# One program per engine across four phases, with the norm's scaling moved to ScalarE

## What is computed

```python
x = x + _L0_xattn_ref(_layernorm(x, axis=-1), ctx_4096, mask_BxSxS2_bk0, ...)   # 32 heads of 128
x = x + _L0_ffn_ref(_layernorm(x, axis=-1), ...)                                # 512 -> 1376 -> 512
x = x + _L1_xattn_ref(_layernorm(x, axis=-1), ctx_4096, ctx_4096, ...)          # 32 query, 8 key heads
x = x + _L1_ffn_ref(_layernorm(x, axis=-1), ...)                                # 512 -> 512, low-rank part
```

```python
def _layernorm(x, axis=-1, eps=1e-05):
    m = jnp.mean(x, axis=axis, keepdims=True)
    v = jnp.var(x, axis=axis, keepdims=True)
    return (x - m) / jnp.sqrt(v + eps)
```

## Time and profile before

| what | us |
| --- | --- |
| three runs | 1722.76, 1722.99, 1725.99 |
| median | 1722.99 |
| the profiled execution | 1721.07 |
| its span, first to last instruction | 1719.3 |
| TensorE busy | 1674.7 |
| VectorE busy | 875.0 |
| ScalarE busy | 647.2 |
| GpSimd busy | 683.0 |

### The profile page before, as it was taken

How to read it: one execution, slowest core, us unless ns; L and a number is a source line. 1 busy time by engine, 2 the same in 40 slices (tenths; PEclk the granted TensorE clock), 3 DMA queues, 4 the chain that set the end, 5 groups by cost and what they waited for, 6 DMA issues and landing times. The chain is left out here.

```text
span 1719.3 us, 26202 instructions
## 1 busy us (share of the span) xinstructions
PE 1674.7 (97%) x9420; PEld 1448.9 (84%) x9420; DVE 875.0 (51%) x1454; ACT 647.2 (38%) x1765; POOL 683.0 (40%) x481
## 2 busy tenths in 40 slices
PE   8999999999999999999989999799999999999997
PEld 7888888888888888888868886688898788888875
DVE  5543444434444344443454345656657556675674
ACT  6432223322233222332322222456556455664550
POOL 4622244322443324433253433445445444443524
PEclk9999999999999999999989999899999999999998
DMA  5110110101101011010011110101011110010011
GB/s 204 53 52 27 52 52 24 52 27 52 52 25 51 30 49 52 29 47 34 1 56 49 43 38 25 65 32 37 32 38 43 45 37 31 25 44 25 27 36 49
DMA packets 30899, 75.00 MB, mean 44 GB/s; under 512 B 5776, under 2 KB 10256, under 8 KB 30832
## 3 DMA queue, kind: packets, MB, share of 16 engines
q1 hardware_dynamic: 30832, 74.10, 12.5%
HBM read 71.99 MB, written 2.10 MB: 43 GB/s over the span
## 5 line engine op out<-in xcount | busy, mean ns | idle before, releaser
L934 POOL TENSOR_TENSOR x_probs<-x_probs,x_inv 128x512 f32<-128x512 f32 x64 | 66.6, 1041 | 461.9 <-DVE x_inv L781 461.9
L1763 POOL TENSOR_TENSOR g_swapped<-g_swapped,rawB 128x512 f32<-128x512 f32 x80 | 103.4, 1294 | 196.9 <-ACT g_swapped L1550 196.9
L637 ACT COPY x_pT<-banks 128x512 f32<-128x512 f32 x64 | 37.4, 586 | 335.6 <-PE banks L486 335.6
L55 PE MATMUL banks<-wtV_hi,cT_lo 128*128 128x256 f32 x512 | 145.3, 284 | 0.0
L57 PE MATMUL banks<-wtV_hi,cT_hi 128*128 128x256 f32 x512 | 144.9, 283 | 0.0
L56 PE MATMUL banks<-wtV_lo,cT_hi 128*128 128x256 f32 x512 | 144.8, 283 | 0.0
L789 DVE COPY x_k<-banks 128x512 f32<-128x512 f32 x60 | 41.5, 692 | 135.6 <-PE banks L57 135.6
L789 DVE COPY x_v<-banks 128x512 f32<-128x512 f32 x60 | 41.5, 692 | 127.7 <-PE banks L57 127.7
L55 PE MATMUL banks<-wtV_hi,g_att_lo 128*128 128x512 f32 x256 | 104.9, 410 | 0.0
L813 DVE TENSOR_TENSOR resid<-banks,resid 128x512 f32<-128x512 f32 x128 | 84.1, 686 | 40.0 <-PE banks L57 40.0
L629 ACT ACTIVATE x_probs<-x_probs,x_top 128x128 f32<-128x128 f32 x256 | 99.2, 390 | 13.1 <-DVE x_top L772 13.1
(11 more groups left out here) (229 smaller groups left out, 4911.7 us busy)
## 6 DMA issues: line engine op xcount, KB each, us to landing
rawV<-in_x_wV SPq DMA_DIRECT2D x16, 512.0 KB, 3.2
rawO<-in_x_wO SPq DMA_DIRECT2D x16, 512.0 KB, 4.0
rawO<-in_g_wQ SPq DMA_DIRECT2D x16, 512.0 KB, 3.2
rawV<-in_g_wO SPq DMA_DIRECT2D x16, 512.0 KB, 3.2
rawA<-in_x_wA SPq DMA_DIRECT2D x15, 512.0 KB, 4.6
rawB<-in_x_wB SPq DMA_DIRECT2D x15, 512.0 KB, 3.2
rawA<-in_f_gu SPq DMA_DIRECT2D x5, 512.0 KB, 3.5
rawB<-in_f_gu SPq DMA_DIRECT2D x5, 512.0 KB, 3.3
```

Of the source, the lines that this page charges most:

```text
L55: pe.matmul(out, w[1], x[0], start=start, stop=False)
L637: nc.scalar.copy(pT[:, j, :], banks[:, TURN_BANK + j, :]).then_inc(pT_ready, 1)
L934: pool.tensor_tensor(probs[:, part, :], probs[:, part, :], rows, ALU.mult).then_inc(probs_ready, 1)
L1763: pool.tensor_tensor(part, part, sin[:, :].unsqueeze(1).to_broadcast([P, HB, P]), ALU.mult)\
```

## The change

The four blocks become one. Each phase is now an object with one function per engine (`Phase`), and each engine runs the four functions in a row; there is no barrier between them. Waits across a border go by semaphores that one phase hands to the next as hooks. The norm's scaling is done by ScalarE (`normalise`, activation Identity with scale `rstd` and bias `shift`), and GpSimd computes `shift` = -mean * rstd in a third one-column instruction. The orders at the borders are written anew. The diff, leaving out changes of indentation and what only renames:

```diff
-    def reciprocal_std(self, pool, b):
+    def factors(self, pool, b):
...
+        pool.wait_ge(self.rstd_ready, b + 1)
+        pool.tensor_scalar(core.shift[:, one], core.moments[:, b, 0:1], core.rstd[:, one], -1.0, ALU.mult, ALU.mult)\
+            .then_inc(self.shift_ready, 1)
-    def add_rows(self, pool):
+    def add_row(self, pool, b):
...
+        pool.wait_ge(self.normed_ready, b + 1)
...
-    def scale(self, dve, b):
+    def normalise(self, act, b):
...
-        dve.tensor_scalar(core.normed[:, b % 2, :], core.resid[:, b, :], core.moments[:, b, 0:1],
-                          core.rstd[:, b:b + 1], ALU.subtract, ALU.mult).then_inc(self.normed_ready, 1)
+        core.nc.scalar.activation(core.normed[:, b % 2, :], core.resid[:, b, :], ACT.Identity,
+                                  bias=core.shift[:, b:b + 1], scale=core.rstd[:, b:b + 1]).then_inc(self.normed_ready, 1)
```

Border 1, from phase 1 to 2 (TensorE, ScalarE, VectorE, GpSimd), and the first chunk of phase 2 on TensorE:

```diff
-                pv(tail, 0, 1, PAIRS - 1)
-                pv(tail, 1, 1, PAIRS - 1)
...
-                norm.weave_tensor(pe, lambda b: output_batch(PAIRS, b))
+            first_head(0)
+            first_head(1)
+            pv(tail, 0, 1, PAIRS - 1)
+            first_head(2)
+            pv(tail, 1, 1, PAIRS - 1)
+            first_head(3)
+            pe.wait_ge(att_lo, 4 * PAIRS - 1)
+            for b in range(B):
+                if b < HB:
+                    output_part(b, 1).then_inc(proj_ready, 1)
+                else:
+                    output_batch(PAIRS, b)
+                if b >= 3:
+                    norm.turn(pe, b - 3)
...
-                norm.weave_scalar(act)
+            after.split_hi(act, used)
+            for b in range(B + 2):
+                if b < B:
+                    norm.normalise(act, b)
+                if b >= 2:
+                    norm.high(act, b - 2)
...
-                norm.weave_vector(dve, lambda b: output_batch(PAIRS, b))
+            for b in range(B):
+                output_batch(PAIRS, b)
+                norm.statistics(dve, b)
+                if b >= 3:
+                    norm.low(dve, b - 3)
+                norm.mean_and_variance(dve, b)
+            for b in range(B - 3, B):
+                norm.low(dve, b)
...
-                after.split_lo(pool)
                 weights("O", PAIRS - 1)
-                norm.weave_gpsimd(pool)
-    return norm
+            after.split_lo(pool)
+            for b in range(B):
+                norm.factors(pool, b)
...
+            def first():
+                pe.wait_ge(gu_hi, 1)
+                pe.wait_ge(gu_lo, 1)
+                before.hooks["added"](pe, 4)
+                pe.wait_ge(before.norm.lo_ready, HB)
+                gate_up(0, 0, 0)
+                before.norm.turn(pe, 5)
+                before.hooks["added"](pe, 6)
+                gate_up(0, 0, 2)
+                before.norm.turn(pe, 6)
+                before.norm.turn(pe, 7)
+                before.hooks["added"](pe, 7)
+                pe.wait_ge(before.norm.lo_ready, B)
+                gate_up(0, 0, 1)
+                gate_up(0, 0, 3)
...
-                before.add_rows(pool)
+            for b in range(B):
+                before.norm.add_row(pool, b)
                 loop(pool, body)
```

Border 2, from phase 2 to 3. The down products and their adds are run from phase 3, between the keys and values of round 0; the turns use two banks:

```diff
+            def start():
...
+                last_down(pe, 0)
+                last_down(pe, 1)
...
+                key(0)
+                last_down(pe, 2)
+                last_down(pe, 3)
+                key(1)
+                norm2.turn(pe, 0)
+                last_down(pe, 4)
+                norm2.turn(pe, 1)
...
+                value(0, 0)
+                last_down(pe, 5)
+                norm2.turn(pe, 2)
+                last_down(pe, 6)
+                norm2.turn(pe, 3)
+                value(0, 1)
+                last_down(pe, 7)
+                norm2.turn(pe, 4)
+                value(0, 2)
+                norm2.turn(pe, 5)
+                norm2.turn(pe, 6)
+                value(0, 3)
+                norm2.turn(pe, 7)
...
+                norm2.high(act, 1)
+                norm2.normalise(act, 3)
+                value_hi(0, 0)
+                norm2.high(act, 2)
+                norm2.normalise(act, 4)
```

Border 3, from phase 3 to 4. The fold of the low-rank weights is made in two halves among the last turns, and the last product of a batch (`final`) stands between the outputs:

```diff
+    def tensor(pe):
...
             for b in range(B):
+            before.hooks["last_output"](pe, b)
+            if b >= 3:
+                norm.turn(pe, b - 3)
+            if b >= 4:
+                final(b - 4)
+        for b in range(4, B):
+            if b >= 5:
+                norm.turn(pe, b)
+            final(b)
...
+    def gpsimd(pool):
+        lora.split_w_lo(pool, 0)
+        lora.split_w_lo(pool, 1)
+        norm.factors(pool, 0)
+        lora.split_w_lo(pool, 2)
+        norm.factors(pool, 1)
+        lora.split_w_lo(pool, 3)
+        for b in range(2, B):
+            norm.factors(pool, b)
+            norm.add_row(pool, b - 2)
...
+        for b in range(5, B):
+            norm.low(dve, b)
+            final(b - 2)
+        final(B - 2)
+        final(B - 1)
```

More of the change, by code:

```diff
@@ L1013, in cross_attention_phase @@
-    return norm
+                twice_of()
+                pool.wait_ge(mask_in, DMA)
+                pool.tensor_scalar(mask[:, :, :], mask8[:, :, :], MASKED, -MASKED, ALU.mult, ALU.add)\
+                    .then_inc(mask_ready, 1)
+                pool.wait_ge(mask_ready, 1)
+                pool.wait_ge(ctx_lo, DC)
+                bias(0, 0, True)
+                normalise(0, 0)
+                normalise(0, 1)
+                weights("A", 1)
+                bias(1, 1)
+                weights("O", 0)
@@ new lines, in body @@
+            def body(g, first, last):
+                a = 2 * g
+                normalise(a - 1, 0)
+                normalise(a - 1, 1)
+                bias(a, 0)
+                weights("V", g)
+                weights("B", g)
+                normalise(a, 0)
+                normalise(a, 1)
+                if not last:
+                    weights("A", g + 1)
+                    weights("O", g)
+                bias(a + 1, 1)
+            start()
+            loop(pool, body)
+            normalise(HEADS - 1, 0)
@@ L1138, in _, with gate_up @@
-                loop(pe, body)
+                    down_batch(pe, c, par, b)
+            def gate_up(c, par, n):
+                m = rows(c)
+                which, half = n // 2, n % 2
+                for k in range(DC):
+                    at = (which * DC + k) * m
+                    mm = product(pe, banks[0:m, n, :], [w[:, at:at + m] for w in gu[par]],
+                                 [s[:, k, half * HALF:(half + 1) * HALF] for s in xT], k == 0, k == DC - 1)
+                mm.then_inc(proj_ready, 1)
@@ new lines, in body, with down_batch @@
+            def body(c, par, turn):
+                pe.wait_ge(gu_hi, c + 1)
+                pe.wait_ge(gu_lo, c + 1)
+                for n in range(4):
+                    pe.wait_ge(hidden_ready, 2 * c - 2 + n % 2 + 1)
+                    gate_up(c, par, n)
+                down(c - 1, 1 - par)
+            first()
+            body(1, 1, 0)
+            loop_rest(pe, body)
+        def down_batch(pe, c, par, b):
+            m = rows(c)
+            product(pe, banks[:, down_bank(c, b), :], [s[0:m, par, tok(b)] for s in hid],
+                    [w[0:m, 0:D] for w in dn[par]], True, True).then_inc(proj_ready, 1)
@@ new lines, in scalar, with gpsimd @@
+    def scalar(act):
+        for b in range(B + 2):
+            if b < B:
+                norm.normalise(act, b)
+            if b >= 2:
+                norm.high(act, b - 2)
+    def gpsimd(pool):
+        lora.split_w_lo(pool, 0)
[7 more added lines that the diff above has]
+            norm.add_row(pool, b - 2)
+        norm.add_row(pool, B - 2)
+        norm.add_row(pool, B - 1)
@@ new lines, in vector, with final @@
+    def vector(dve):
+        def final(b):
+            dve.wait_ge(out_ready, b + 1)
+            dve.wait_ge(norm.row_added, b + 1)
+            dve.tensor_tensor(resid[:, b, :], bank(b), resid[:, b, :], ALU.add).then_inc(added, 1)
+        for b in range(B):
+            before.hooks["last_add"](dve, b)
+            norm.statistics(dve, b)
+            if b >= 3:
+                norm.low(dve, b - 3)
+            norm.mean_and_variance(dve, b)
+            if b >= 5:
+                final(b - 5)
+        for b in range(5, B):
+            norm.low(dve, b)
+            final(b - 2)
+        final(B - 2)
+        final(B - 1)
```

2327 lines of the change are left out of this document (1198 added, 1129 removed).

## The result

| kernel | median us | range | ratio to the kernel before (95%) |
| --- | --- | --- | --- |
| before | 1722.99 | 1721.48 to 1725.99 | |
| changed | 1713.24 | 1711.17 to 1715.18 | 0.9945 (0.9933 to 0.9956) |

A forecast was written before the change was run, and what follows sets the result against it. TensorE, busy 97% of the span, was taken as the bound, with only idle and lower-clock time winnable. Borders summed -6 + 17.5 + 1.5 = 13.0 us gained, giving 1710 us; 1702 to 1717 for this case, 8 in 10 within 1699 to 1719.

The forecast's parts named there:

- Border 1: First border between phases, up to chunk 1: 6 us lost, bounds 3 and 9 lost.
- The ring: Border 1: each batch circles through aggregate, GpSimd's var, pow and shift, normalise, high and low, 3.4 us against 2.31 before.
- The nine slow matmuls: Before chunk 1 at border 1: an idle stretch of some 3 us, then nine lower-clock matmuls, up to 1.9 us more.
- Border 2: From the last chunk's first product to the first key product: 17.5 us gained, bounds 13 and 19.5.
- the cover: Border 2: key halves and value blocks placed between the turns give TensorE work, so nearly all of its waits are hidden.
- the loss at pv: When round 0 begins behind border 2: ScalarE's fuller queue moves the next pair's pv ready time by up to 0.8 us.
- Border 3: Last border, outputs to the last add: 1.5 us gained, bounds 4 gained and 4 lost.
- I take off 0.9: Border 3: slow matmuls behind idle stretches of 2.2 to 3 us cut the gain from 2.4 to 1.5 us.
- all low bounds together: Sum over the three borders if each meets its low bound: stated as 5 us gained.
- A: Rival: the ring doesn't bind and ScalarE's chain keeps TensorE's pace at borders 1 and 3, about 1692 us; 10%.
- B: Rival: the last border stays at 1.2 GHz (18 us lost), chunk 0 likewise (5 later), 1733 us; 7%.
- C: Rival: border 2 only half covered, late normed holds several turns and the clock falls, 1715 to 1718 us; 10%.

The follow-up runs named there:

- The filled kernel: Changed kernel plus 36 extra matmuls with unread results in TensorE's idle stretches ahead of finals 0, 5, 6 and 7 at border 3: 1706.44 us, ratio 0.9912.
- the swap experiment: Changed kernel with ScalarE running high(b-2) ahead of normalise(b), not behind it, at borders 1 and 3: 1700.92 us, ratio 0.9870.
- the kernel with the scaling on VectorE: Changed kernel with the norm's scaling back on VectorE at all three borders and no shift on GpSimd: 1705.64 us, ratio 0.9898.
- the kernel without the cover: Changed kernel with border 2's last down products, norm and turns ahead of round 0's keys and values, query-weight split behind all factors: 1724.83 us, ratio 1.0013.

## Why the prediction came out as it did

The forecast was 1710 us in a range of 1699 to 1719; measured 1713.24. Case by case, on the stretches:

- **Border 1, forecast 6 lost, measured 5.1** between the cuts (4.1 in the start of chunk 1, by which I had reckoned; 1.1 us were won ahead of the border). The ring was worked out at 3.4 us and is 3.44; its parts were right too: shift 0.27 taken and 0.27 measured, normalise 0.80 taken from line 683 and 0.81 measured. Start of chunk 1 forecast 901.4, measured 901.0; that it is this near is in part luck, since these 1.1 us are in it. The nine slow matmuls that I added before chunk 1 (1.9) did not come: after 1.5 us of idle time its matmuls start 0.23 apart. Not seen by me: ScalarE's cast of wtB_hi ends 0.3 us later than the row adds that I had as the last term, and is a second bound.
- **Border 2, forecast 17.5 gained, measured 17.3** up to the query product of the second pair, 12.8 of it by the cover, by an experiment. But the forecast had the loss at pv in it, and it was too small there: put at 0.8, it is a wait of 3.1 us for `g_pT_lo` at 1124, and 3.8 in all. In the forecast's own terms border 2 gained 13.5, 4 less. The trace shows which chain ends last in this wait (GpSimd's weight split, sine, `g_q`, `g_pT_lo`), and the wait is as long without the cover. That it was hidden before by the value products, which then stood between the first query products and now stand ahead of them, is only argued.
- **Border 3, forecast 1.5 gained, measured 3.2 lost** (front and rest, 60.15 before and 63.36 after). Here lies the term that was mis-sized most. The order was right: outputs 2.9 us sooner (3 forecast), final 0 starts 12.6 us after the first output (11.7 forecast), waits before finals 5 to 7 of 2.9, 2.1 and 2.1 (3.0, 2.2, 2.2 forecast). What failed is the step "I take off 0.9" for slow matmuls behind these waits. The filled kernel puts them at 4.7, since they came three times, in finals 0, 5 and 7. I had priced them at 1.9 for one stretch from the earlier trace rows, behind an idle time of 1.8 us, and then charged half of one where the same text named three stretches. The other 0.9 of the miss is in final 0, which came 0.9 later than forecast from the first output.
- **The sum.** -5.1 + 17.3 - 3.2 = 9.0, and 0.9 that the borders don't explain: 1.1 ahead of border 1, 0.6 in the chunks, -0.8 in the rounds, which are the 3.8 lost at pv and 3.0 won behind it. The span is 9.9 us shorter. One sum of the prediction is wrong: all low bounds together (-9 + 13 - 4) gain 0 us, not 5; neither forecast nor range was taken from it.
- **Rivals.** A (the ring doesn't bind) is excluded by the 3.44 us and by the swap experiment. B (the lower clock at the end) happened in small: not 28 us of work at the lower level but some eight matmuls three times. The mechanism was there, but between the waits the clock came back each time. C (border 2 half covered) did not happen: one wait of 0.2 us up to the last turn. The changed kernel loses behind the border, and by less than C has it.

That the total lay only 3.2 us from the forecast is in part luck. Border 2 with what hangs on it came 4.0 us worse than forecast and border 3 4.7 worse. Against them stand border 1, 0.9 better, and 4.7 us that I had not forecast at all: 1.1 ahead of border 1, 0.6 in the chunks, and 3.0 in the rounds, of which 2.2 are the clock at one place in the two executions.

## What to carry to other kernels

When work moves from one in-order queue to another, follow one item round all queues and write down over how many items the circle spans, before counting busy time: here a circle over one batch ran at 3.44 us for each, with VectorE idle for 1.4 of them, and with two swapped instructions it was 1.98 with VectorE busy throughout. An instruction that needs the result of the latest item should stand behind those that serve older items. And price each idle stretch of TensorE twice, with itself and with the slow matmuls behind it, for each stretch anew.

## What the hardware showed

Idle stretches of 2 to 3 us on TensorE are not followed by the lower clock every time. Behind 3.18 us (final 0) three matmuls came 0.23 us apart, then eight 0.42 apart. Behind 2.85 (final 5) the first seven were slow at once, behind 2.09 (final 6) none, behind the next 2.09 (final 7) the last eight. Behind 1.49 at chunk 1 there was none. Nor is 1.9 us, the price in the earlier trace rows, the most that follows one stretch. Behind the wait for `g_pT_lo`, 3.1 us in both, the kernel with the scaling on VectorE ran 20 us at a mean granted clock of 0.85, which costs 3 us, and the changed kernel at 1.00 (windows, in this order):

```profile
1120.00:1140.00 20.00, 19.89 (x107) 17.91 (x107) 14.23 (x20) 10.18 (x31) 5.09 (x4) 0.85 0.12 40
```

```profile
1124.00:1144.00 20.00, 19.96 (x119) 17.71 (x120) 16.88 (x25) 12.51 (x46) 6.70 (x5) 1.00 0.12 41
```

So the price of a single stretch can't be read from its length; here it lay between 0 and 3 us. Extra matmuls without a use, put into the same stretches, brought all of it to the higher level and the end 4.7 us nearer.

A small instruction on GpSimd can be stretched beside a large one of VectorE. In the changed kernel's border 2 the one-column `var_eps` takes 0.58 us twice, at 1073.41 and at 1078.26, where its six other batches there take 0.22:

```profile
1073.41 0.58 POOL L176 TENSOR_SCALAR var_eps<-moments 128x1 f32<-128x1 f32 x1 [0.97 <-DVE moments L169]
...
1075.54 0.22 POOL L176 TENSOR_SCALAR var_eps<-moments 128x1 f32<-128x1 f32 x1 [0.53 <-DVE moments L169]
```

Both start beside the same kind of VectorE instruction, the add of line 1791 at 1073.24 and at 1078.09, which has two inputs and none of them from the banks. In the kernel without the cover, where no `var_eps` starts beside this add, none is stretched. Which rule is behind it no run here tells.
